# An audio tower on one core: the loops of `pipeline` and `rounds` written out

## The chip, the core and the metric

The kernel runs on one core of a Trainium2 chip. The metric is the time of one execution on the device, in microseconds (us). Each engine of the core runs its own program: TensorE (PE, with its weight loads shown as PEld), VectorE (DVE), ScalarE (ACT), GpSimd (POOL) and SyncE (SP), which here only issues DMA transfers. The engines are ordered against each other by semaphores: an instruction raises one when it is done, another waits until it has reached a value.

## The reference, cut to what matters

The input `x` is 16 batches of 64 channels by 2048 samples. Three stages follow each other.

```python
h = _L0_tok_ref(x, ...)                        # token stage: (16, 128, 1024)
h = h + _L0_attn_ref(_layernorm(h), ...)       # attention stage
h = h + _L0_ffn_ref(_layernorm(h), ...)        # feed-forward stage

# token stage
h = conv1d(x, conv_in_w, pad=3)                # 7 taps, 64 -> 128 channels
h = gelu(groupnorm1(h, gn1_w, gn1_b))
h = conv1d(h, dw_w, stride=2, pad=2, groups=H) + dw_b     # 5 taps, by channel
h = gelu(groupnorm1(conv1d(h, pw_w), gn2_w, gn2_b))       # 128 -> 128

# attention: 32 heads, latent queries (384) and keys (128), rotary part of 64
q_c = rmsnorm(hidden @ w_qa, g_qa); q = q_c @ w_qb
kv = hidden @ w_kva                            # k_c (128, normed) and k_rope (64)
attn = softmax((query @ key.T) * scaling); out = (attn @ v) @ w_o

# feed-forward: a dense layer, and 8 experts of rank 16, the best 2 for each token
out = x @ W_base.T + b_base + sum_of_two_experts(x) * 2
```

## The kernel before, in words

All matrices are split into two halves of 16 bits, a high and a low one (`_h`, `_l`), and most products are made of three matmuls (high by high, low by high, high by low). `resid` holds the running result of all 16 batches in SBUF.

**Token stage** (`token_phase`). One iteration `i` of a pipeline works on several batches at once: the convolution of batch `i`, the first group norm and gelu of `i - 1` (MID), the second of `i - 2` (HID), the layer norm's turned result and the projections of `i - 3` (PROJ), the latents of `i - 4` (TAIL), and the splitting of the input of `i + 2` (AHEAD; `x_high` on ACT, `x_low` on POOL). PE, DVE, ACT and POOL each run `pipeline` (L64) with a body of their own. `pipeline` writes out the iterations at the start and the end, where some of the lags are out of range, and runs the middle, here iterations 4 to 13, as a hardware loop `Fori` whose pass holds two iterations. In the loop the iteration number is a register, and so are the values that waits compare with; in the iterations written out both are constants, and `need` and the bodies' `isinstance(i, int)` leave out waits that can't matter. `wait_apart` (L82) and `Chain` put waits between small operations on one engine. The small steps of the norms on POOL go by `Chain`, as do the sums on DVE (`mean_and_square`). `kr_l` (L405 on DVE) is the last operation of an iteration there. SP loads `x` in a loop of its own (`sp.Fori(1, B)`).

**Attention stage** (`attention_phase`). A round is one group of four heads by one of four quads of batches, 32 rounds in all (`ROUNDS`). A round has four steps `j`. In each step PE makes the scores of one batch for four heads (`scores`, L1068 to L1075, which need `zt`, the rotary queries transposed by DMA), the latent outputs of the step before (`latents`, L1110 to L1112, which need `turned`, the probabilities transposed by DMA), the rotary queries of the next step (`rope`, L1041), a quarter of the queries of the next round (`queries`, L1025), in the first 28 rounds some products of weights for a head four rounds on (`products`), and the output of the step before (`outputs`, L1090 to L1092). DVE and ACT do the softmax and all splitting; SP issues the transposes (L784 `zt`, L791 `turned`), in a loop of its own over all 128 steps (`sp.Fori(1, ROUNDS * QUAD - 1)`). At the start of a round ACT issues the load of another head's weights (`load`, L836), from round 0 to round 26. `rounds` (L758) sets the order for PE, ACT and DVE: round 0 written out, rounds 1 to 26 in a loop of two rounds a pass, round 27 written out, rounds 28 to 30 in a loop of one round a pass, round 31 written out. Where the round is a register, `Round` and `fresh` (L660 to L664) compute the slot, group, side, token offset and half that the round needs by register operations on each engine, anew where an operand needs one.

**Feed-forward stage** (`ffn_phase`). One iteration for each batch: SP transposes the normed input and stores the result, DVE routes, PE multiplies. All five engines run `pipeline`, with iterations 2 to 13 (SP, ACT, DVE) or 2 to 15 (PE, POOL) in the loop.

Of the kernel before, what the change touches and what calls it, by code (L numbers as in the profile page):

```python
# [22 lines left out]
B, CI, T, CH = 16, 64, 2048, 128  # L23
# [11 lines left out]
HEADS = 4  # L35
# [3 lines left out]
ROUNDS = GROUPS * QUADS  # L39
# [22 lines left out]


def pipeline(eng, body, first, lags, steady, unroll=2):  # L64

    assert steady >= max(lags)
    lo, hi = steady, B + min(lags)
    hi -= (hi - lo) % unroll  # L70
    for i in range(first, lo):
        body(i, i % 2, lambda lag, i=i: 0 <= i - lag < B)
    with eng.Fori(lo, hi - unroll + 1, unroll) as r:
        for u in range(unroll):
            body(r + u if u else r, (lo + u) % 2, lambda lag: True)
    for i in range(hi, B + max(lags)):
        body(i, i % 2, lambda lag, i=i: 0 <= i - lag < B)


# [39 lines left out]
def token_phase(nc, keep, raw_loaded, x_d, wc_d, wqk_d, pw_d, rows_d, params_d, consts_d, heads_d):  # L119
# [4 lines left out]
    with ExitStack() as ctx:  # L124
# [101 lines left out]
        def _(act):  # L226
# [95 lines left out]
            weights_high("wc")  # L322
            act.wait_ge(zeroed, ZEROED)
            pipeline(act, body, AHEAD, lags, TAIL)

        @block.gpsimd
        def _(pool):
# [67 lines left out]
            pool.wait_ge(zeroed, ZEROED)  # L395
            pool.wait_ge(w_loaded["params"], 16)
            pipeline(pool, body, AHEAD, lags, TAIL)

        @block.vector
        def _(dve):  # L400
# [152 lines left out]
            dve.wait_ge(zeroed, ZEROED)  # L553
            dve.wait_ge(w_loaded["params"], 16)
            pipeline(dve, body, -1, lags, TAIL)

        @block.tensor
# [155 lines left out]
def attention_phase(nc, keep, raw_loaded, heads_d):  # L713
# [3 lines left out]
    with ExitStack() as ctx:  # L717
# [40 lines left out]
        def rounds(eng, start, body):  # L758

            def run(t, more, parity=None):  # L760
                def at(k):
                    if isinstance(t, int) and not 0 <= t + k < ROUNDS:
                        return None
                    return Round(eng, t + k if k else t, parity if k == 0 or parity is None else 1 - parity)

                body(at(-1), at(0), at(1), more)

            start()
            run(0, True)
            with eng.Fori(1, ROUNDS - HEADS - 2, 2) as t:  # L770
                run(t, True, 1)
                run(t + 1, True, 0)
            run(ROUNDS - HEADS - 1, True)
            with eng.Fori(ROUNDS - HEADS, ROUNDS - 1) as t:
                run(t, False)
            run(ROUNDS - 1, False)

        @block.sync
        def _(sp):
# [22 lines left out]
        def _(act):  # L802
# [52 lines left out]
            def body(before, now, after, more):  # L855
# [25 lines left out]
                if not after:  # L881
                    latent_high(now.slot + (QUAD - 1), False)

            rounds(act, start, body)

        @block.vector
        def _(dve):
# [67 lines left out]
            def body(before, now, after, more):  # L955
# [33 lines left out]
                if not after:  # L989
# [3 lines left out]
                    dve.wait_ge(out_added, ROUNDS * 8)  # L993

            rounds(dve, start, body)

        @block.tensor
        def _(pe):
# [115 lines left out]
            def body(before, now, after, more):  # L1114
# [18 lines left out]
                if not after:  # L1133
                    latents(now, QUAD - 1)
                    outputs(now, QUAD - 1)

            rounds(pe, start, body)


# [350 lines left out]
```

## Time and profile before

| | before |
|---|---|
| median of 3 runs | 2132.52 us (2131.76 to 2133.24) |
| the profiled execution | 2130.34 us |
| its span, first to last instruction | 2128.6 us |
| PE busy | 1938.4 us, 91% of the span, 11794 matmuls |
| DVE busy | 1314.6 us, 62% |
| ACT busy | 757.9 us |
| POOL busy | 279.4 us |
| mean granted TensorE clock | 0.974 of full speed |

The profile is of one execution. A busy time counts an engine's own instructions; register, branch, semaphore and DMA-issuing instructions are not counted as busy. Matmuls overlap, so a busy PE is not PE at its peak. Idle time before an instruction is put down to what ended it; "issue" means that nothing which the profile shows was waited for.

### The profile page before, as it was taken

The numbers are of one execution on the slowest core, as the hardware profiler recorded it, in microseconds if no ns is written. First come the engines' busy times: TensorE is split into PE (matmuls) and PEld (weight loads), VectorE is DVE, ScalarE is ACT, GpSimd is POOL, SyncE is SP. The second block draws the span as 40 slices with busy tenths as digits, with TensorE's granted clock in tenths as the row PEclk, the third lists the DMA queues.
The fourth block names the chain that finished last, engine by engine and source line by source line (L and its number), as shares of the span: only waits on it lengthen the run. The fifth ranks groups of instructions, "written<-read, shape, count | busy, mean of one in ns | idle before, by whom it ended". The sixth has DMA issues, their size and how long they took to land. (4 is left out here: it accounts for less than half of the span.)

```text
span 2128.6 us, 42839 instructions
## 1 busy us (share of the span) xinstructions
PE 1938.4 (91%) x11794; PEld 1066.4 (50%) x11794; DVE 1314.6 (62%) x2805; ACT 757.9 (36%) x2051; POOL 279.4 (13%) x612
## 2 busy tenths in 40 slices
PE   4788888768999999999999999999999999959999
PEld 1344445444555555555555555555555555525554
DVE  3666666635666666666666666666666666656664
ACT  3344444323333333333333333333333333332221
POOL 2354444320000000000000000000000000023332
PEclk8899999979999999999999999999999999979999
DMA  5112211003332222222232222322222121243332
GB/s 137 40 40 47 49 42 38 19 3 95 55 68 55 55 55 69 54 52 54 55 73 55 55 52 54 69 55 55 55 67 55 37 43 38 40 137 75 83 80 69
DMA packets 250560, 123.82 MB, mean 58 GB/s; under 512 B 240272, under 2 KB 240528, under 8 KB 248336
## 3 DMA queue, kind: packets, MB, share of 16 engines
q1 hardware_dynamic: 246192, 94.71, 20.7%
q10 hardware_dynamic: 4320, 28.51, 4.3%
q8 instruction: 25, 0.41, 0.1%
q14 instruction: 23, 0.19, 0.0%
HBM read 56.07 MB, written 8.39 MB: 30 GB/s over the span
## 5 line engine op out<-in xcount | busy, mean ns | idle before, releaser
L1090 PE MATMUL out_ps<-m_h,ot_h 128*128 (+1 forms) x1024 | 389.0, 380 | 4.1 <-DVE ot_l L889 4.1
L1092 PE MATMUL out_ps<-m_h,ot_l 128*128 (+1 forms) x1024 | 388.8, 380 | 0.0
L1091 PE MATMUL out_ps<-m_l,ot_h 128*128 (+1 forms) x1024 | 388.7, 380 | 0.0
L939 DVE SCALAR_TENSOR_TENSOR resid<-out_ps,resid 128x512 f32 (+1 forms) x256 | 177.1, 692 | 309.7 <-PE out_ps L1092 308.6
L804 ACT ACTIVATE ot_h<-av_ps 128x512 f16<-128x512 f32 x128 | 76.4, 597 | 762.5 <-PE av_ps L1112 762.5
L1281 POOL MEMSET fpower<- 128x1 f32 x1 | 0.1, 99 | 1426.3 <-POOLq L717 1426.3
L868 ACT ACTIVATE prob<-s_ps,nmx 128x128 f32<-128x128 f32 x512 | 180.1, 371 | 5.7 <-DVE nmx L965 5.7
L1090 PEld LDWEIGHTS out_ps<-m_h,ot_h 128*128 128x128 f16 x1024 | 100.4, 98 | 129.9 <-issue 13.9
L1091 PEld LDWEIGHTS out_ps<-m_l,ot_h 128*128 128x128 f16 x1024 | 100.4, 98 | 129.5 <-issue 19.1
L1092 PEld LDWEIGHTS out_ps<-m_h,ot_l 128*128 128x128 f16 x1024 | 100.3, 98 | 121.2 <-issue 0.8
L960 DVE TENSOR_REDUCE mx<-s_ps 128x4 f32<-128x512 f32 x128 | 88.5, 692 | 63.9 <-PE s_ps L1075 63.9
L889 DVE SCALAR_TENSOR_TENSOR ot_l<-av_ps,ot_h 128x512 f16<-128x512 f32 x128 | 88.5, 692 | 63.3 <-ACT ot_h L804 63.3
L889 DVE SCALAR_TENSOR_TENSOR halves<-prob,halves 128x512 f16<-128x512 f32 x128 | 88.6, 692 | 59.5 <-ACT halves L804 59.5
L1025 PE MATMUL qp_ps<-qct_h,wp_h 128*128 (+1 forms) x378 | 103.3, 382 | 21.1 <-issue 21.1
L868 ACT ACTIVATION_READ_ACCUMULATOR prob<-s_ps,nmx 128x1 f32 x512 | 109.0, 213 | 0.0
L1025 PE MATMUL qp_ps<-qct_h,wp_l 128*128 (+1 forms) x378 | 102.5, 380 | 0.0
L1025 PE MATMUL qp_ps<-qct_l,wp_h 128*128 (+1 forms) x378 | 102.2, 379 | 0.0
L1394 PE MATMUL fout<-wb_h,fht_h 128*128 128x512 f16 x256 | 97.1, 379 | 0.0
L1394 PE MATMUL fout<-wb_l,fht_h 128*128 128x512 f16 x256 | 97.1, 379 | 0.0
L1394 PE MATMUL fout<-wb_h,fht_l 128*128 128x512 f16 x256 | 97.1, 379 | 0.0
L804 ACT ACTIVATE halves<-prob 128x512 f16<-128x512 f32 x128 | 80.6, 630 | 44.3 <-DVE prob L973 44.3
L1068 PE MATMUL s_ps<-kct_h,qp_h 128*128 (+1 forms) x512 | 92.4, 219 | 0.4 <-DVE qp_l L889 0.4
(239 smaller groups left out, 4014.5 us busy)
## 6 DMA issues: line engine op xcount, KB each, us to landing
wide<-heads_in ACTq DMA_DIRECT2D x30, 928.0 KB, 5.4
wide<-x_in SPq DMA_DIRECT2D x32, 512.0 KB, 6.0
tower_out<-result SPq DMA_DIRECT2D x16, 512.0 KB, 2.6
stage<-wb_in SPq DMA_DIRECT2D x8, 512.0 KB, 8.3
resid<-wqk_in SPq DMA_DIRECT2D x1, 2304.0 KB, 11.8
zt<-z SPq DMA_TRANSPOSE x128, 2.4
turned<-halves SPq DMA_TRANSPOSE x128, 3.0
wide<-heads_in SPq DMA_DIRECT2D x2, 928.0 KB, 4.6
```

The costliest lines, as they stand in the source:

```text
L804: act.activation(out, src, ACT.Copy, scale=scale).then_inc(done, 1)
L868: act.activation(prob[:, h, :], s_ps[:, h * P:(h + 1) * P], ACT.Exp, bias=nmx[:, h:h + 1], scale=EXP_SCALE, accum_out=rsum[:, h:h + 1]).th ...
L889: dve.scalar_tensor_tensor(out=out, in0=src, scalar=scale, in1=high, op0=ALU.mult, op1=ALU.subtract).then_inc(done, 1)
L939: dve.scalar_tensor_tensor(out=resid[:, at], in0=out_ps[hf][:, :], scalar=1.0 / (O_S * M_S), in1=resid[:, at], op0=ALU.mult, op1=ALU.add). ...
L960: dve.tensor_reduce(mx[:, :], s_ps[:, :].rearrange("p (h n) -> p h n", h=HEADS), AX.X, ALU.max).then_inc(max_step, 1)
L1025: last = pe.matmul(bank[:, :], w[:, bass.ds(side, 1), k, j, :].rearrange("p a n -> p (a n)"), q[:, k, bass.ds(tok, CHUNK)], start=n == 0, ...
L1068: pe.matmul(out[h], q_h[h], k_h, start=h == 0, stop=False)
L1090: pe.matmul(out_ps[hf][:, :], ot_h[:, h, :], m_h[:, at], start=h == 0, stop=False)
L1091: pe.matmul(out_ps[hf][:, :], ot_h[:, h, :], m_l[:, at], start=False, stop=False)
L1092: last = pe.matmul(out_ps[hf][:, :], ot_l[:, h, :], m_h[:, at], start=False, stop=h == HEADS - 1)
L1281: pool.memset(power[:, :], -0.5).then_inc(powered, 1)
L1394: pe.matmul(out_ps[p][hf][:, :], h[p][:, k, :], w[:, k, hf * CHUNK:(hf + 1) * CHUNK], start=k == 0 and n == 0, stop=False)
```

## The change

`pipeline` no longer has a middle part: each iteration from `first` on is written out by the program that builds the kernel, with its number as a constant. `rounds` does the same for the 32 rounds. The `Fori` loops of both are gone, on every engine that calls them; SP's own two loops, in the token and the attention stage, stay. The operations and their order on each engine are as before.

```diff
 def pipeline(eng, body, first, lags, steady, unroll=2):
-    assert steady >= max(lags)
-    lo, hi = steady, B + min(lags)
-    hi -= (hi - lo) % unroll
-    for i in range(first, lo):
-        body(i, i % 2, lambda lag, i=i: 0 <= i - lag < B)
-    with eng.Fori(lo, hi - unroll + 1, unroll) as r:
-        for u in range(unroll):
-            body(r + u if u else r, (lo + u) % 2, lambda lag: True)
-    for i in range(hi, B + max(lags)):
+    for i in range(first, B + max(lags)):
         body(i, i % 2, lambda lag, i=i: 0 <= i - lag < B)
...
             start()
-            run(0, True)
-            with eng.Fori(1, ROUNDS - HEADS - 2, 2) as t:
-                run(t, True, 1)
-                run(t + 1, True, 0)
-            run(ROUNDS - HEADS - 1, True)
-            with eng.Fori(ROUNDS - HEADS, ROUNDS - 1) as t:
-                run(t, False)
-            run(ROUNDS - 1, False)
+            for t in range(ROUNDS):
+                run(t, t < ROUNDS - HEADS)
```

## Rows read from the trace of the kernel before

**Rows 1.** Windows, attention rounds: stretch, width, busy us (instructions) by engine, PE clock, DMA
```profile
541.40:631.70 90.30, 85.45 (x541) 47.22 (x540) 55.98 (x120) 31.71 (x104) 0.00 (x0) 1.00 0.31 57
...
631.70:1684.20 1052.50, 1019.32 (x6482) 567.20 (x6481) 670.04 (x1440) 377.48 (x1248) 0.00 (x0) 1.00 0.26 57
1684.20:1726.50 42.30, 41.99 (x272) 23.56 (x271) 27.91 (x60) 15.69 (x52) 0.00 (x0) 1.00 0.20 38
1726.50:1845.00 118.50, 118.50 (x782) 66.34 (x781) 78.33 (x168) 42.27 (x144) 0.00 (x0) 1.00 0.22 40
```

**Rows 2.** Windows (PE, PEld, DVE, ACT, POOL), the loop of the feed-forward stage
```profile
1949.10:2107.20 158.10, 158.10 (x949) 82.11 (x948) 95.42 (x226) 34.14 (x48) 58.41 (x106) 1.00 0.31 80
```

**Rows 3.** Waits of PE, 631.7 to 1684.2: total us, times, longest us
```profile
PE qp_ps L1025 <- issue: 18.9, 24, 0.8
PE s_ps L1074 <- DMA zt<-z: 9.6, 23, 0.6
PE av_ps L1110 <- DMA turned<-halves: 3.9, 19, 0.2
```

**Rows 4.** Timeline of PE in round 27: start, us, instruction [idle before, releaser]
```profile
1695.62 0.38 PE L1110 MATMUL av_ps<-turned,kc_h 128*128 128x512 f16 x1 [0.31 <-DMA turned<-halves]
1695.84 0.38 PE L1111 MATMUL av_ps<-turned,kc_l 128*128 128x512 f16 x1
```

**Rows 5.** Timeline of PE in round 17, first query matmuls
```profile
1250.44 0.81 PE L1025 MATMUL qp_ps<-qct_h,wp_h 128*128 x3 [0.78 <-issue]
```

**Rows 6.** Source line L663 (`fresh`), whole span: ns min/median/max, first and last start
```profile
L663 PEldq FUSED_REGOPS  x584: 47/157/245, 542.4 to 1836.9; - x195
```

**Rows 7.** Timeline of ACT, the load of a head at the turn to round 18
```profile
1284.96 0.35 ACTq L836 DMA_DIRECT2D wide<-heads_in  x1
```

**Rows 8.** Tile `zt`, 1284.5 to 1285.5: its transpose and its landing
```profile
L784 SPq DMA_TRANSPOSE zt<-z x1: 1191/1191/1191, 1284.7 to 1284.7; - x1
...
DMA to landing us min/median/max: 6.0/6.0/6.0
```

**Rows 9.** DMA, 631.7 to 1684.2: all queues with packets; issues, median us to landing
```profile
q1 hardware_dynamic: 154649, 38.03, 19.3%
q10 hardware_dynamic: 3331, 21.92, 6.6%
...
zt<-z SPq DMA_TRANSPOSE x96, 2.4
```

**Rows 10.** DMA, 1684.2 to 1767: instruction queues, packets, MB, share of 16 engines
```profile
q8 instruction: 5, 0.08, 0.4%
q14 instruction: 4, 0.03, 0.1%
```

**Rows 11.** DMA, 541.4 to 631.7 (rounds 1 and 2): instruction queues
```profile
q8 instruction: 6, 0.10, 0.5%
q14 instruction: 3, 0.02, 0.1%
```

**Rows 12.** Tile `zt`, 1690 to 1690.5: the transpose on SP's queue, ns
```profile
L784 SPq DMA_TRANSPOSE zt<-z x1: 2252/2252/2252, 1690.0 to 1690.0; - x1
```

**Rows 13.** Tile `zt`, 580.5 to 581.5: landing of the one transpose there
```profile
DMA to landing us min/median/max: 7.9/7.9/7.9
```

**Rows 14.** Windows, token stage: nine loop steps, then two steps written out
```profile
132.30:361.17 228.87, 195.86 (x1062) 108.28 (x1062) 149.13 (x315) 105.14 (x172) 108.56 (x253) 0.96 0.18 41
361.17:408.54 47.37, 38.45 (x224) 22.07 (x224) 32.61 (x70) 19.76 (x36) 19.91 (x55) 1.00 0.12 41
```

**Rows 15.** Source line L87 (waits of `wait_apart`), POOL: ns min/median/max
```profile
L87 POOLq FUSED_REGOPS  x375: 37/46/57, 107.5 to 2095.8; - x188
```

**Rows 16.** Timeline of DVE: `kr_l` at 132.30, 361.17 and 408.54
```profile
132.30 0.29 DVE L405 SCALAR_TENSOR_TENSOR kr_l<-turn_ps,kr_h 128x128 f32 x1 [3.14 <-ACT kr_h L319]
...
361.17 0.29 DVE L405 SCALAR_TENSOR_TENSOR kr_l<-turn_ps,kr_h 128x128 f32 x1 [3.10 <-ACT kr_h L319]
...
408.54 0.29 DVE L405 SCALAR_TENSOR_TENSOR kr_l<-turn_ps,kr_h 128x128 f16<-128x128 f32 x1 [2.85 <-ACT kr_h L319]
```

## The prediction, made blind

> **What bounds the kernel now.** The page comes first: its first part names TensorE as by far the busiest engine, VectorE next. Those are means over three stages, so I then cut the span into windows, one for each stretch in which a loop runs and one for each stretch of the same work that is already written out. The reader should compare their width with PE's busy time. The loop over attention rounds 3 to 26 takes 1052.50 us for 24 rounds, 43.85 us each, with PE busy for 42.47 of them; round 27, which the kernel before already writes out on PE, ACT and DVE, takes 42.30 us with PE busy for 41.99; rounds 28 to 30, which have no products and still run in a loop, are 118.50 of 118.50 us busy [rows 1]. The loop of the feed-forward stage is full too: 158.10 of 158.10 us [rows 2]. So there is nothing to gain in rounds 28 to 30 and in the feed-forward loop, where PE never waits for a register; what can be gained lies in rounds 1 to 26 and in the token stage.
>
> In the 24 rounds PE has three idle groups: 18.9 us before `qp_ps` L1025 with "issue" as the cause, 9.6 us before `s_ps` L1074 for the transposed `zt`, 3.9 us before `av_ps` L1110 for `turned` [rows 3]. By round these are 0.79, 0.40 and 0.16 us. The idle time of PE understates a stall: matmuls of that shape last 0.38 us and start 0.22 us apart [rows 4], so each stop costs about 0.16 us more than is shown.
>
> The "issue" stall comes once a round, 0.78 us ahead of the first query matmul [rows 5]. It is the helper `fresh` (L663): 584 fused register operations on PE's queue, median 157 ns [rows 6]. Where `queries` turns to the next round's registers, several of these operations follow each other with no matmul between.
>
> The `zt` stall belongs to another cause. At the turn of each round ACT issues the load of another head's weights [rows 7]; the `zt` transpose issued beside it lands after 6.0 us [rows 8], where the median of the 96 is 2.4 us [rows 9]. PE needs that `zt` at the start of the round. The load stays in the changed kernel, so most of this stall is not the loop's.
>
> **The change, part by part.** The sum is made against the profiled execution, 2130.3 us (span 2128.6); the median of the runs is 2132.5, so I add 2.2 us at the end.
>
> *Attention, rounds 1 to 26: registers and back edges removed.* The nearest row is round 27, 42.30 us [rows 1]. It contains one stop of its own, 0.31 us idle before L1110 [rows 4], with the restart 0.47 us, so a round without any stop is 42.30 - 0.47 = about 41.85 us. Round 27 lacks one thing that rounds 1 to 26 have, the load. What the load costs in the loop is 0.40 + 0.16 us idle and two restarts, 0.85 us [rows 3, 4]. In the trace the load is issued 0.3 us after `zt` (1284.96 against 1284.7) [rows 7, 8], with register moves ahead of it on ACT. Without these I expect it some 0.3 us earlier, and since `zt` lands when the load does, the stall should shrink to about 0.4 us. Bounds: 0.1 and 0.85.
>
> *Attention: instruction blocks added.* This is the price of the change. While the loop runs (631.7 to 1684.2) the DMA view names only queues q1 and q10: not one instruction packet in 24 rounds [rows 9]. Wherever code runs for the first time there are such packets: 5 on q8 and 4 on q14 in the 82.8 us from round 27 on [rows 10], 6 and 3 in rounds 1 and 2 [rows 11], about four and a half a round. Written out, all rounds are of that kind. The packets don't stop PE's queue itself (the rows of round 27 to 30 show no issue stall) but they share DMA engines with the transposes: the `zt` transpose issued at 1690.0 took 2252 ns on SP's queue [rows 12] against 1191 ns for the one at 1284.7 [rows 8], and the `turned` behind it is what PE then waited 0.31 us for [rows 4]. With the load in the way as well it is worse: the `zt` at the turn to round 2, issued at 580.7, landed after 7.9 us rather than 6.0 [rows 8, 13]. From below: round 27 lost 0.47 us to four packets or so, and rounds 28 to 30 nothing to the others; call it 0.2 us a round. From above: rounds 1 and 2 together took 90.30 us [rows 1], 2.6 us more than two later ones, for nine packets, so 0.29 us each and 1.3 us a round; 1.5 with some margin. A packet hurts when it falls into the 7 us or so around the load, one sixth of a round, which four or five packets will do in most rounds without the full 1.9 us each. I take 0.8, between the ends and nearer to rounds 1 and 2, as they alone have load and packets together.
>
> Sum for a round: 41.85 + 0.4 + 0.8 = 43.05 us, 26 rounds 1119.3. Before they took 90.30 + 1052.50 = 1142.8 us [rows 1]. Gain 23.5 us; with the bounds of both terms from 42.15 to 44.2 us a round, that is from 47 us gained to 6 lost.
>
> The Trainium skill (Runtime: NRT & Kernel Launch, Instruction fetch mechanics) has a rule on this: prefetch is sequential, and a taken branch whose target lies outside a window of two blocks stalls for a fetch, which speaks for writing loops out more strongly than I do. The trace disagrees here, since the loop's twelve passes fetched nothing [rows 9]; by the rule twelve further stalls would vanish, each about as long as a q8 packet (0.4% of 16 engines' time in 82.8 us for five, 1.1 us each [rows 10]), and the sum would be near 2082.
>
> *Rounds 28 to 30 and the feed-forward loop.* No stall to remove [rows 1, 2]; new packets meet transposes there that are issued well ahead and no load. I take 0.5 us lost, at most 2.
>
> *Token stage, iterations 4 to 13.* Here PE is not the limit: it is busy for 195.86 of 228.87 us in the loop [rows 14]. One chain goes round through all engines: `kr_l` on DVE, the sums of the next batch, `stat_ps` on PE, the group norm's small steps on POOL, the gelu on ACT, five taps on DVE, the layer norm on POOL, `hid` on ACT, `kr_l` again. Between its links sit register operations for the waits: 375 in all on POOL for L87 alone, median 46 ns, and the like on DVE [rows 15]. `kr_l` runs at 132.30 and 361.17 with nine loop steps between, 25.43 us each; the two steps after, to 408.54, which are written out already, take 23.69 each [rows 16], 1.74 us less. They lack only the load-ahead `x_high` and `x_low`, which in the loop fill gaps on ACT and POOL. Part of the 1.74 us is TensorE's clock: in the loop it is granted at 0.96 of 2.4 GHz on the mean, with falls to 1.2 GHz, and at 1.00 in the two steps [rows 14]. PE has its waits for this chain before each fall, so a shorter chain should see fewer; I don't count on all. I take 1.4 us for ten steps, 14 us; bounds 7 and 17. The chain uses no DMA transposes, so packets cost it nothing.
>
> *What stays.* SP's own loops in the token and attention stages (`sp.Fori` over batches and over the 128 transposes) are not touched, and their register work stays in the path of `zt`. No matmul, copy or load is added or dropped.
>
> Sum: 2130.3 - 23.5 - 14 + 0.5 = 2093.3 us; on the median's footing 2095.5, say 2095.
>
> **The rivals.**
> - *Packets are hidden and the load moves out of the way.* Round 27 nearly shows it, but it has no load. Then a round is 42.1 us, 26 rounds gain 48, the token stage 17: 2132.5 - 65 = about 2068. The page cited above says that crossing a block boundary is mostly hidden, which would be this case; rounds 1 and 2 speak against it.
> - *Attention gives its gain back.* Each round loses its 0.95 us of register stall to packets on the load, that is 1.7 us of packets a round. Only the token stage gains: 2132.5 - 14 = about 2118.
> - *Slower.* The place is the first `zt` of each round. If packets fall on the load in every round as at 580.7, each round pays 1.9 us there and some 0.5 in later steps: 41.85 + 0.4 + 2.4 = 44.65, times 26 is 1161, 18 us more than before; with the token stage at its low bound of 7 the time is about 2143. It decides from 2.25 us of packets a round, where the token gain of 14 is used up. Against it: with a packet every 10 us or so, not every one can fall into those 7 us.
> - *It does nothing.* If the written-out waits cost as much as the registers did, the time stays at 2132; round 27 speaks against it plainly.
>
> **How the numbers follow.** Forecast about 2095 (2082 to 2108): 0.57. Packets hidden: 0.13. Attention gives back: 0.17. Slower: 0.08. No change: 0.05. A measurement of this kernel tells 0.2%, 4.3 us, from no change. So faster 0.87, same 0.05, slower 0.08. The range 2070 to 2124 holds the forecast, the third case and part of the second, and leaves out most of the slower ones.
>
> **What would show each step.** Right: the issue group before L1025 is gone; rounds of about 43 us with PE idle only at L1074 and L1110; instruction packets in every round; the load issued no later than `zt`; steps of about 24 us between `kr_l`. Wrong: "issue" idle on PE at regular places (the fetch itself stalls it), rounds over 43.9 us with a longer `zt` wait, or token steps that stay at 25.4 with the clock still falling.

## The result, and the profile after

The changed kernel takes 2095.93 us (median of 4 runs, 2090.39 to 2096.80) against 2132.14 us before: ratio 0.9825, 95% interval 0.9807 to 0.9842. The prediction was 2095 us, 2070 to 2124. The profiled execution took 2096.29 us for a span of 2094.5 us, 34.0 us less than the profiled one before.

The lines of the helpers moved up: L1025, L1074 and L1110 of before are now L1008, L1057 and L1093, the load L836 is L819, and `kr_l` L405 is L394. The windows that answer to [rows 1] and [rows 14] are, in the order rounds 1 to 26, round 27, rounds 28 to 30, nine token steps that were a loop, and the two after them (columns as in those groups: width, busy us of PE, PEld, DVE, ACT and POOL, clock, DMA):

```profile
528.30:1650.50 1122.20, 1101.87 (x7022) 615.76 (x7021) 725.57 (x1560) 408.19 (x1352) 0.00 (x0) 1.00 0.29 59
1650.50:1692.30 41.80, 41.80 (x271) 23.56 (x270) 27.89 (x60) 15.69 (x52) 0.00 (x0) 1.00 0.20 39
1692.30:1810.80 118.50, 118.50 (x782) 66.23 (x781) 77.91 (x168) 42.27 (x144) 0.00 (x0) 1.00 0.21 41
...
131.99:347.53 215.54, 184.32 (x1062) 104.37 (x1062) 150.11 (x316) 105.22 (x171) 117.31 (x253) 1.00 0.19 45
347.53:394.82 47.29, 38.40 (x224) 22.07 (x224) 32.80 (x71) 19.77 (x36) 20.29 (x55) 1.00 0.12 41
```

Rounds 1 to 26 took 1142.8 us before [rows 1] and take 1122.2 now: 20.6 us gained, 43.16 us a round. The nine token steps took 228.87 us [rows 14] and take 215.54: 13.3 us. The two together are 33.9 of the 34.0 us; the rest of the program moved by 0.1 us. The clock in the token steps is 1.00 where it was 0.96.

PE's waits in rounds 1 to 26, which answer to [rows 3] (total us, times, longest), are these two groups alone:

```profile
PE s_ps L1057 <- DMA zt<-z: 10.2, 13, 1.7
PE av_ps L1093 <- DMA turned<-halves: 9.5, 28, 0.4
```

Over the same 26 rounds of the kernel before ([rows 3] has 24 of them) they were

```profile
PE qp_ps L1025 <- issue: 21.1, 28, 0.8
PE s_ps L1074 <- DMA zt<-z: 12.0, 25, 2.2
PE av_ps L1110 <- DMA turned<-halves: 4.1, 20, 0.2
```

The "issue" group is gone. The wait for `zt` is little shorter, but comes half as often: 6.6 of its 10.2 us now fall on four rounds, 1.6 to 1.7 us in each. The wait for `turned` has more than doubled. The DMA view of the same stretch, which answers to [rows 9], now has instruction packets (packets, MB, share of 16 engines), some two of PE's (q8) in each round:

```profile
q8 instruction: 56, 0.92, 0.3%
q14 instruction: 30, 0.25, 0.1%
...
wide<-heads_in ACTq DMA_DIRECT2D x25, 928.0 KB, 5.3
```

They don't cost all rounds the same. A round is counted here from its first score matmul to the next round's. Twenty-two rounds take 42.3 to 43.3 us; rounds 6, 12, 18 and 24 take 44.2, 45.8, 45.8 and 45.8. Rounds 11 and 12 as windows, in the columns of the first fence:

```profile
957.60:999.90 42.30, 41.95 (x271) 23.57 (x270) 27.90 (x60) 15.70 (x52) 0.00 (x0) 1.00 0.27 59
999.90:1045.80 45.90, 43.94 (x272) 24.27 (x271) 27.99 (x60) 15.79 (x52) 0.00 (x0) 0.96 0.31 56
```

Ahead of round 12 the load is issued at 995.02 (from ACT's timeline: start, us), 0.04 us before the `zt` transpose at 995.06, and that `zt` lands after 7.3 us (from the view of the tile); ahead of round 11, with the same 0.04 us, it took 5.5:

```profile
995.02 0.33 ACTq L819 DMA_DIRECT2D wide<-heads_in  x1
```
```profile
L767 SPq DMA_TRANSPOSE zt<-z x1: 1189/1189/1189, 995.1 to 995.1; - x1
...
  PE s_ps L1057: 1.6, 1
...
DMA to landing us min/median/max: 7.3/7.3/7.3
```

The DMA view of the 1.2 us from the start of round 12 on, 999.9 to 1001.1, has one packet of PE's instructions, while `zt` was still on its way. The same stretch of round 11 has none.

```profile
q8 instruction: 1, 0.02, 4.8%
```

So three things were to be tested: whether the two gains are apart from each other, what in a round costs the 1.3 us above a round without stops, and what makes the token steps shorter.

### The profile page after: what moved, and what is told of

Same layout as the page of the kernel before. It is cut to its first block and busy times, and to the rows that moved or that the text cites. A ratio compares the mean times of both kernels' runs of the same rounds, so it can differ in the third digit from the quotient of the medians.

```text
span 2094.5 us, 33517 instructions
## 1 busy us (share of the span) xinstructions
PE 1924.3 (92%) x11794; PEld 1064.8 (51%) x11794; DVE 1310.3 (63%) x2805; ACT 755.6 (36%) x2051; POOL 286.4 (14%) x612
## 3 DMA queue, kind: packets, MB, share of 16 engines
q1 hardware_dynamic: 246192, 94.71, 21.7%
## 5 line engine op out<-in xcount | busy, mean ns | idle before, releaser
L1073 PE MATMUL out_ps<-m_h,ot_h 128*128 128x512 f16 x1024 | 388.2, 379 | 4.1 <-DVE ot_l L872 4.1
L1075 PE MATMUL out_ps<-m_h,ot_l 128*128 128x512 f16 x1024 | 388.1, 379 | 0.0
L1074 PE MATMUL out_ps<-m_l,ot_h 128*128 128x512 f16 x1024 | 388.1, 379 | 0.0
L922 DVE SCALAR_TENSOR_TENSOR resid<-out_ps,resid 128x512 f32<-128x512 f32 x256 | 177.0, 691 | 285.4 <-PE out_ps L1075 281.4
L1074 PEld LDWEIGHTS out_ps<-m_l,ot_h 128*128 128x128 f16 x1024 | 100.2, 98 | 129.2 <-issue 18.6
L1008 PE MATMUL qp_ps<-qct_h,wp_h 128*128 128x512 f16 x378 | 104.8, 387 | 0.0
L1008 PE MATMUL qp_ps<-qct_h,wp_l 128*128 128x512 f16 x378 | 102.7, 381 | 0.0
L1008 PE MATMUL qp_ps<-qct_l,wp_h 128*128 128x512 f16 x378 | 102.1, 379 | 0.0
L1051 PE MATMUL s_ps<-kct_h,qp_h 128*128 128x128 f16 x512 | 92.4, 219 | 0.4 <-DVE qp_l L872 0.4
```

Of the source, the lines that this page charges most:

```text
L922: dve.scalar_tensor_tensor(out=resid[:, at], in0=out_ps[hf][:, :], scalar=1.0 / (O_S * M_S), in1=resid[:, at], op0=ALU.mult, op1=ALU.add). ...
L1008: last = pe.matmul(bank[:, :], w[:, bass.ds(side, 1), k, j, :].rearrange("p a n -> p (a n)"), q[:, k, bass.ds(tok, CHUNK)], start=n == 0, ...
L1051: pe.matmul(out[h], q_h[h], k_h, start=h == 0, stop=False)
L1073: pe.matmul(out_ps[hf][:, :], ot_h[:, h, :], m_h[:, at], start=h == 0, stop=False)
L1074: pe.matmul(out_ps[hf][:, :], ot_h[:, h, :], m_l[:, at], start=False, stop=False)
L1075: last = pe.matmul(out_ps[hf][:, :], ot_l[:, h, :], m_h[:, at], start=False, stop=h == HEADS - 1)
```

## Experiments on the two parts

**The token stage alone, and the rounds alone.** On the kernel before, a copy of `pipeline` without its loop serves the token stage's four engines, or `rounds` is written out, and nothing else:

```diff
+def pipeline_out(eng, body, first, lags, steady, unroll=2):
+    for i in range(first, B + max(lags)):
+        body(i, i % 2, lambda lag, i=i: 0 <= i - lag < B)
...
-            pipeline(act, body, AHEAD, lags, TAIL)
+            pipeline_out(act, body, AHEAD, lags, TAIL)
```

> The kernel before, with only the token stage's batch pipelines written out on all four engines. Theory (the change's gain is the sum of two parts that don't touch): the token stage gains about 13 us, as between the two traces, and the attention rounds keep their 43.85 us each, so about 2132 - 13 = 2119 us; kr_l steps fall from 25.4 to about 23.9 us, and no fall of PE's clock between 113 and 396 us. Rival (the gain of the attention rounds needs the token stage to be written out too, or the token's gain is lost later, since rounds that start elsewhere collide otherwise): outside 2115 to 2123 us.

Measured: 2120.45 us, ratio 0.9938 (0.9917 to 0.9960) to the kernel before at 2133.53 on the same chip, so the time came as expected. The clock did not: the profile has three falls, at 280.67, 304.57 and 328.46 us, and nine token steps in 218.05 us.

> The kernel before, with only the attention rounds written out on PE, ScalarE and VectorE; the token and feed-forward pipelines stay loops. Theory: the rounds gain 20.6 us, as between the two traces, and the token stage nothing, so about 2111 us, rounds of 43.16 us in the mean; the load is issued right before the zt transpose, and instruction packets of PE come back in every round. The slow rounds (44.2 to 45.8 us in the changed kernel: 6, 12, 18 and 24) stay six rounds apart, but may fall on other rounds, since PE has run another number of instructions by then. Rival (the slow rounds belong to the rounds' own work or loads): they stay 6, 12, 18 and 24.

Measured: 2111.86 us, ratio 0.9903 (0.9877 to 0.9928). The two gains, 13.1 and 21.7 us, add to 34.8; the changed kernel gained 36.2. The parts are apart. And the slow rounds moved: with the rounds alone written out they are 3, 9, 15 and 21 (43.7 to 45.9 us). Rounds 9 and 15 of that kernel, behind all of its rounds 1 to 26:

```profile
543.10:1661.50 1118.40, 1098.76 (x7021) 614.29 (x7020) 725.45 (x1560) 408.10 (x1352) 0.00 (x0) 1.00 0.29 59
886.40:930.80 44.40, 42.10 (x271) 23.56 (x270) 27.89 (x60) 15.70 (x52) 0.00 (x0) 1.00 0.30 59
1144.80:1190.80 46.00, 43.93 (x272) 24.29 (x271) 27.99 (x60) 15.70 (x52) 0.00 (x0) 0.96 0.30 56
```

**PE's rounds alone.** As before, but `rounds` is written out for PE only (`rounds(pe, start, body, True)`), so ScalarE keeps its loop and issues the load behind `zt`.

> The kernel before, with the attention rounds written out on PE alone; ScalarE and VectorE keep their loops, so the load of the next head is still issued by ScalarE after its register work, 0.3 to 0.6 us behind the zt transpose. Theory A (PE's own register work is all of the gain, and PE's instruction packets the loss): 0.7 to 0.95 us less in each round for the issue stall, the same packets, so about 2111 us, as with all three engines. Theory B (the load's earlier issue is part of the gain or of the loss): if the zt transpose that starts ahead of the load lands in 6.0 us or less, the rounds become shorter than with all three engines, 2105 us or less; if the load behind it costs more in the turned transposes, longer, 2116 us or more.

Measured: 2117.71 us (2109.87 to 2119.67), ratio 0.9933 (0.9911 to 0.9954); the profiled execution is the fastest of the four. In it the load is issued 0.28 and 0.62 us behind `zt` by turns, rounds 1 to 26 take 1119.3 us against 1118.4 with all three engines written out, and PE's waits are

```profile
PE s_ps L1078 <- DMA zt<-z: 16.6, 24, 2.1
PE av_ps L1114 <- DMA turned<-halves: 4.3, 21, 0.3
```

20.9 us together against 19.4 (9.6 and 9.8) with all three engines. In the same stretch the DMA view has

```profile
q8 instruction: 57, 0.93, 0.4%
q14 instruction: 3, 0.02, 0.0%
```

where the changed kernel has 56 and 30, so the packets on q8 are PE's. The profile speaks for theory A: half a microsecond in the load's place moves waiting between `zt` and `turned` and saves nothing. The median, 6 us above the three engines' with intervals that overlap, leans to the slower half of theory B. That stays open.

## Experiments on the round: load and instruction packets

**The load cut in four.** The changed kernel, with the round's 928 KB in four pieces by columns, one at the start of each step, and PE's wait for the load counting all four:

```diff
-            def load(h, p):
-                act.dma_start(raws[p][:, 0:RAW], heads_d[bass.ds(h, 1), :, :].rearrange("a p n -> (a p) n")
+            def load(h, p, part=None):
+                lo, hi = (0, RAW) if part is None else (part * RAW // 4, (part + 1) * RAW // 4)
+                act.dma_start(raws[p][:, lo:hi], heads_d[bass.ds(h, 1), :, lo:hi].rearrange("a p n -> (a p) n")
...
-                    load(now.t + HEADS + 1, 1 - now.parity)
                 for j in range(QUAD):
                     s = now.slot + j
+                    if more and (not now.known or now.t + HEADS + 1 < NH):
+                        load(now.t + HEADS + 1, 1 - now.parity, j)
```

> The changed kernel with each round's load of 928 KB cut in four loads of 232 KB by columns, one issued at the start of each of the round's four steps instead of all at the first. Theory (what a round has left above 41.85 us is the load lying on the zt and turned transposes, and an instruction packet of PE that comes on top of both in every sixth round): the first zt lands in about 3 us instead of 5.5 to 7.3, the rounds 6, 12, 18 and 24 are like the others, no fall of PE's clock between 510 and 1800 us, rounds of 42.0 to 42.4 us, so about 20 to 30 us less than the changed kernel: 2066 to 2076 us. Rival 1 (the instruction packets alone hold PE up, without the load): rounds stay near 43 and the time at 2090 or more. Rival 2 (four loads hit four zt and four turned transposes instead of one, and each is late by a little): no gain or a loss, 2095 us or more.

Measured: 2063.62 us, ratio 0.9675 (0.9659 to 0.9691), below the 2066 to 2076 us expected. Its rounds 1 to 26, PE's waits in them, and the DMA view of the same stretch:

```profile
536.30:1627.40 1091.10, 1089.82 (x7022) 613.49 (x7021) 725.72 (x1560) 408.09 (x1352) 0.00 (x0) 1.00 0.30 61
```
```profile
PE av_ps L1096 <- DMA turned<-halves: 1.2, 5, 0.3
```
```profile
q8 instruction: 56, 0.92, 0.3%
q14 instruction: 31, 0.25, 0.1%
...
wide<-heads_in ACTq DMA_DIRECT2D x103, 232.0 KB, 2.7
zt<-z SPq DMA_TRANSPOSE x104, 3.2
```

A round takes 41.96 us in the mean, 41.86 in most, with the same 56 packets on q8 as in the changed kernel. So with the load cut the packets cost 0.1 us a round, and the other 1.2 us (43.16 - 41.96) need the whole load. Both rivals fall. A packet still delays a `zt` here: in rounds 6, 12, 18 and 24, where one of PE's starts 1.3 to 2.3 us ahead of the round, that `zt` lands 5.6, 4.9, 5.2 and 4.8 us after its issue, and in the other rounds after 3.2 to 3.8. But PE reaches its first `zt` matmul 5.5 us after the issue, so only round 6, with 42.3 us, pays for it. With the whole load `zt` takes 5.4 us or more in every round, so that time is used up.

**The same cut on the kernel before.**

> The kernel before with the same cut of the load in four, loops kept: the price of the load alone, where PE has no instruction packets in rounds 4 to 25. Theory: PE's wait for zt (9.6 us) and for turned (3.9 us) in rounds 1 to 26 goes, and little else, while ScalarE gets three more sets of address registers and DMA issues in a round: 13 us less at most, 2119 to 2127 us. Together with the changed kernel this gives the parts of a round: without packets and without the load's collision, with either, with both. Rival (the issue stall behind the register work covers the same time as the load's wait): less than 4 us gained.

Measured: 2094.24 us, ratio 0.9824 (0.9808 to 0.9840): as much as the whole change, three times the most I had expected. Rounds 1 to 26 and PE's only wait in them:

```profile
543.30:1646.90 1103.60, 1093.17 (x7021) 612.86 (x7020) 726.00 (x1560) 408.34 (x1352) 0.00 (x0) 1.00 0.29 59
```
```profile
PE qp_ps L1028 <- issue: 10.4, 28, 0.6
```

The waits for `zt` and `turned` are gone, as expected. What I had not expected is that the register stall shrinks too, to 0.40 us a round (0.55 and 0.22 by turns) from 0.79 [rows 3], though the register operations are still there. Their place shows why. First the kernel before in round 17, ahead of the stall of [rows 5]: the operations of L663 on PE's queue (ns min, median, max; first and last start), and PE's first matmul that uses `zt`:

```profile
L663 PEldq FUSED_REGOPS  x6: 93/200/240, 1247.0 to 1249.8; - x6
```
```profile
1246.98 0.23 PE L1074 MATMUL s_ps<-kr_h,zt 128*128 x1 [0.39 <-DMA zt<-z]
```

Then the same round with the load cut, with the first query matmul as well:

```profile
L663 PEldq FUSED_REGOPS  x6: 93/200/240, 1223.0 to 1225.7; - x6
```
```profile
1223.53 0.22 PE L1077 MATMUL s_ps<-kr_h,zt 128*128 x1
...
1226.32 0.81 PE L1028 MATMUL qp_ps<-qct_h,wp_h 128*128 x3 [0.55 <-issue]
```

Six operations of the same lengths over 2.7 to 2.8 us, but with the late `zt` they begin as the `zt` matmul begins, and with the cut load 0.5 us ahead of it. In the program the wait for `zt` stands ahead of these operations on the same queue; while the queue waits, it can't get ahead of the matmuls. Whether it is the size of the four pieces or their place in the round that lets `zt` land in time, these runs don't tell apart.

The four kernels make a table of the mean round in us, and the two causes overlap in it:

| | load whole | load cut in four |
|---|---|---|
| loops | 43.95 | 42.45 |
| written out | 43.16 | 41.96 |

**The packets' place moved.** The changed kernel with 128 more PE instructions before the attention, half of one of PE's packets of 16 KB (in rounds 1 to 26, 14,043 matmuls and weight loads and 390 waits went with 56 packets, about 258 to a packet):

```diff
+                if i >= 16:
+                    for _ in range(32):
+                        pe.sem_inc(pad, 1)
```

> The changed kernel with 128 more PE instructions in the token stage (increments of a semaphore that nobody waits for, 32 in each of the last four iterations, where PE waits for VectorE anyway): half of one of PE's instruction packets of 16 KB, so the packets fall half a period earlier in all that follows. Theory (a round is slow when a packet falls in its first microsecond, on the zt transpose and the load): the slow rounds move from 6, 12, 18 and 24 by three, to 3, 9, 15 and 21, as they lay in the kernel before with the rounds alone written out; the time is 2090 to 2100 us. Rival (the slow rounds belong to the heads or to the load): they stay.

Measured: 2097.89 us, ratio 0.9847 (0.9831 to 0.9864). The slow rounds are 3, 9, 15 and 21 now (44.1, 45.9, 43.9, 43.8). Rounds 6, 9 and 12 of this kernel:

```profile
747.30:789.80 42.50, 42.12 (x271) 23.57 (x270) 27.91 (x60) 15.70 (x52) 0.00 (x0) 1.00 0.29 60
874.70:920.60 45.90, 43.89 (x272) 24.24 (x271) 28.01 (x60) 15.69 (x52) 0.00 (x0) 0.96 0.30 58
1005.80:1048.70 42.90, 42.33 (x272) 23.61 (x271) 27.91 (x60) 15.70 (x52) 0.00 (x0) 1.00 0.27 61
```

The slow rounds follow the count of PE's instructions, not the heads. The start times of the packets in five traces say the same: those of the changed kernel, of this one, of the next, and of the kernels with the rounds written out alone, on three engines or on PE. In 20 of their 130 rounds a packet on q8 starts between 0.2 us before the round's start and 0.9 us after it; these take 43.7 to 45.9 us, with a `zt` that lands after 6.8 to 7.7 us. In the other 110 the rounds take 42.3 to 43.4 us and `zt` 5.4 to 6.7. With 56 packets in 26 rounds, 2.15 a round, a packet comes 0.15 of a period earlier each time, so one falls on the round's start in every sixth or seventh. The 128 instructions turned that by three rounds and left the time as it was.

**SyncE's loops written out as well.**

```diff
-            with sp.Fori(1, B) as b:
+            for b in range(1, B):
...
-            with sp.Fori(1, ROUNDS * QUAD - 1) as s:
+            for s in range(1, ROUNDS * QUAD - 1):
```

> The changed kernel with SyncE's own two loops (the token batches' loads and stores, and the attention's zt and turned transposes) written out too. Theory: SyncE's register work stands between its waits and its issues, so a transpose would be issued some 0.1 to 0.3 us earlier; PE waits for zt and turned in few rounds, so 0 to 5 us less than the changed kernel, 2090 to 2096 us. Rival (SyncE then takes instruction packets of its own, which come on top of its transposes): slower than the changed kernel, 2098 us or more.

Measured: 2097.49 us (2090.76 to 2101.07), ratio 0.9829 (0.9807 to 0.9852): nothing gained that can be measured, between the theory's range and the rival's. Its rounds are 42.94 us, with the slow ones again at 6, 12, 18 and 24, but at 44.1 to 44.3 us, since none of them had a fall of the clock. By that comparison each fall in the changed kernel's slow rounds cost 1.6 us. Its token steps gave back more than the rounds gained (225.83 us for nine, clock 0.92), which leads to the next part.

## Experiments on the token stage

**VectorE's pipeline alone.**

```diff
-            pipeline(dve, body, -1, lags, TAIL)
+            pipeline_out(dve, body, -1, lags, TAIL)
```

> The kernel before, with only VectorE's token pipeline written out; PE, ScalarE and GpSimd keep their loops. Theory (the chain between two kr_l passes crosses all four engines and each of them has register work on it): VectorE's share is what its own pieces lost, dw to lv 0.4 us and the copies 0.1 to 0.3 us, some 0.5 us a step over 10 steps, so about 2127 us (2125 to 2129). Rival 1 (VectorE alone bounds the steps): all 13 us, 2119 us. Rival 2 (the chain's other engines set the step, VectorE's register work runs while it waits): 2132 us.

Measured: 2132.78 us in the median of ten runs, ratio 0.9993 (0.9975 to 1.0010), but three of the ten lie at 2119.5 to 2123.8 us with a mean clock of 0.972 to 0.976, the other seven at 2128 to 2136 with 0.961 to 0.969. The profiled one is the fastest, with nine token steps in 219.10 us. By the median rival 2 would be right, by the profile rival 1. The clock had to be taken out.

**PE's idle time filled.** Each token step has one long idle stretch of PE, mostly 2.3 to 2.7 us before the `stat_ps` matmul, and where the clock fell in a step, it fell within 1.6 us of the end of that stretch (from 2.4 to 1.2 GHz at 183.84 us, with SyncE's loops written out, where PE's idle time ended at 183.81). Ten matmuls whose output nobody reads fill it:

```diff
+                    need(pe, s_copied, i - 1, LAST + HID)
+                    if ok(0) and ok(TAIL):
+                        for _ in range(10):
+                            pe.matmul(stat_ps[:, 4:512], wc_h[:, 0, :], x_h[p][:, 0:508], start=True, stop=True)
                     need(pe, st1_ready, i * 2, 2 * B)
                     need(pe, st2_ready, (i - HID) * 2 + 2, 2 * B)
-                    need(pe, s_copied, i - 1, LAST + HID)
```

> The kernel before, with ten matmuls of 508 columns in each full iteration of the token stage (into columns of stat_ps that nobody reads) at the place where PE stands idle for 2.3 to 2.7 us ahead of the stat_ps matmul; their time is about 10 x 0.216 = 2.2 us, so they fill the idle time and should delay nothing. Theory (a fall of PE's clock follows that idle time, and makes the step that it hits about a microsecond longer; the rest of the token stage's gain is register work): no falls between 130 and 380 us, kr_l steps of 24.9 us (as in the undisturbed ones of the kernel before) instead of 25.4, so 5 us less, 2127 us. Rival 1 (the falls are all of the difference between the two kernels' token stages): 23.9 us a step, 2118 us. Rival 2 (the falls have nothing to do with that idle time, or cost nothing): 2132 us or more.

Measured: 2129.31 us against 2132.75, ratio 0.9983 (0.9973 to 0.9992): less of a gain than the theory's 5 us, but clear of rival 2.

> The kernel before with VectorE's token pipeline alone written out, and the same ten matmuls. That kernel without them came out at 2119.5 to 2123.8 us in three of ten runs and at 2128 to 2136 in the others, with a mean clock of 0.972 to 0.976 against 0.961 to 0.969; its profiled run was the fastest, with kr_l steps of 24.15 us and few falls. Theory (VectorE's register work is worth 1.2 us a step, and falls of the clock after PE's idle time take it back in most runs): with the idle time filled all runs lie at 2117 to 2123 us, steps of 24.2 us or less. Rival (the two levels come from elsewhere): both levels stay, median near 2132 us.

Measured: 2122.40 us (2120.47 to 2127.22), ratio 0.9957 (0.9941 to 0.9974). The median is the theory's, but only two of the four runs lie at 2123 us or less, as all should have.

> The changed kernel with the load cut in four, as before, and the same ten matmuls in the token stage. The cut alone gave 2063.6 us, with 2060.3 to 2074.3 over its runs; the profiled run was the slowest, with a fall of the clock in each token step and steps of 24.5 to 26.5 us. Theory: no fall between 130 and 380 us, steps of 23.7 to 24.3 us in every run, 2058 to 2064 us, and a spread of 4 us or less. Rival (the filling work delays the stat_ps matmul or the conversion behind it): steps of 24.5 us or more, 2066 us or more.

Measured: 2063.59 us (2063.30 to 2065.99), ratio 0.9678 (0.9662 to 0.9694). The median is that of the cut load without the filling; the spread is 2.7 us over four runs instead of 13.9 over five. Nine token steps of these three kernels, in this order, each from its own windows:

```profile
132.41:357.94 225.53, 206.86 (x1155) 113.54 (x1153) 148.92 (x316) 106.34 (x172) 119.19 (x253) 1.00 0.19 42
```
```profile
130.83:348.14 217.31, 206.18 (x1152) 113.26 (x1151) 149.03 (x316) 104.70 (x172) 117.36 (x253) 1.00 0.19 44
```
```profile
130.77:346.96 216.19, 203.77 (x1153) 113.01 (x1152) 150.07 (x316) 105.27 (x171) 117.58 (x253) 1.00 0.20 45
```

In all three the clock is at 1.00 through the steps, where the kernel before has 0.96 [rows 14] and the cut load without filling had

```profile
130.97:355.36 224.39, 199.34 (x1062) 110.54 (x1062) 151.21 (x316) 104.80 (x171) 103.84 (x253) 0.92 0.19 43
```

So the 228.87 us of before come down by 3.3 us without the falls, by 8.2 more with VectorE's register work gone, and by 1.1 with that of PE, ScalarE and GpSimd. These are windows of one profile each; by the medians VectorE's part is 6.9 us (2129.31 to 2122.40). Rival 1 of the run with VectorE's pipeline alone was near: with the falls out, VectorE carries most of the register work's gain. The expectation of 24.9 us a step for the filled kernel before was near (24.9 and 25.2 by turns). With the idle stretch filled, the falls in the steps are gone in all three profiles. The stretch alone doesn't always bring one: the changed kernel's profile has 2.4 to 2.7 us of it in each of the nine steps, and no fall. Whether extra matmuls elsewhere in the step would do the same was not tried.

## Why the prediction was right, step by step

**The round without a stop, 41.85 us.** Right: most rounds of the written-out kernel with the cut load take 41.86.

**The register stall gone from the rounds.** Right in its sign; its size was misread. I took the 0.79 us of "issue" and the 0.40 us for `zt` [rows 3] as two causes that lie side by side. Half of the first came from the second, as the late `zt` took the queue's lead away. Of the 1.50 us that cutting the load saves in the kernel before I had given the load 0.85.

**The load's wait, 0.4 us, and the packets, 0.8 us a round.** The sum was near, 1.2 against 43.16 - 41.86 = 1.30, and that is why the term came out at 20.6 us instead of 23.5. That was luck, since its two parts were mis-sized in opposite ways. With the load cut, packets cost 0.1 us; the whole load with packets around it costs 1.2 more. The step that failed is "packets cost as in rounds 1 and 2, in most rounds": they strike hard where one falls in the first microsecond of a round, which is four rounds of 26. Those four cost 181.7 us, 10.7 more than four of the others' mean, (1122.2 - 181.7) / 22 = 42.75, which is 0.4 us a round over all 26, half of the 0.8; three falls of the clock at 1.6 us are 4.8 of that. What is left, 42.75 - 41.86 = 0.9 us in every round, twice the 0.4, goes with the load, for it went when the load was cut; what the packets elsewhere in a round add to it stays open, as no written-out run has the load without packets. The low end of 0.2 rested on a stop in round 27 that I put down to packets: the changed kernel's round 27 has two on q8 and two on q14 as well, and no stop.

**The load issued 0.3 us earlier.** Right (0.04 us before `zt`, before 0.3 or 0.6 behind it by turns), but it saved nothing in all. In the 22 ordinary rounds `zt` landed a little sooner, after 5.8 us in the median against 6.05 before, and PE waited 0.16 us a round for it instead of the 0.40 of [rows 3]. For `turned` it waited 0.37 us instead of 0.16, so the two together are as long as before. With PE alone written out, where the load stays behind `zt`, they were only 1.5 us longer in 26 rounds than with all three engines.

**Token stage, 14 us.** Right: 13.3 for nine steps in the profile, 13.1 us by the medians of the token stage alone. That the profile agrees so well is luck: it has no fall of the clock in those steps, and the same token code took 217.5, 218.1, 224.4 and 225.8 us in the profiles of four other kernels (128 more PE instructions, token stage alone, load cut, SyncE's loops out). The split between register work and clock was left open in the prediction; it is about 9.3 to 3.3, of the register work 8.2 on VectorE. The low bound of 7 was too high: the changed token stage with falls of the clock in most of its steps took 224.39 us in the profile of the cut load, 4.5 us less than before, and 225.83 with SyncE's loops written out, 3.0 us less.

**Rounds 28 to 30 and the feed-forward stage, 0.5 us lost.** Nothing was lost: from round 27 on the kernels take 444.4 us before and 444.0 after, and round 27 alone went from 42.30 to 41.80.

**The rivals.** The 2068 us of "packets are hidden and the load moves out of the way" describe the cut load well, 2063.6; but the load had to be cut for it, the change alone didn't. "Attention gives its gain back" and "slower" needed a packet on the load in all or most rounds. It is each sixth, because 2.15 packets a round make the collision wander; that a count near a whole number would let it stay is argued, not tried.

The Trainium skill (Runtime: NRT & Kernel Launch, Instruction fetch mechanics) calls the crossing of a block boundary mostly hidden. The runs agree for PE's own queue: with 56 packets PE had no issue stall. The price lay elsewhere, in a `zt` that was late already and landed later still with a packet beside it. The Trainium skill (Trainium Kernel Development and Optimization, Key Constraints) says that DMAs issued from the SP, ACT and POOL queues run on the same 16 DMA engines and interleave. It doesn't name instruction packets there; the DMA view counts them as a share of these 16 engines too (q8 had 4.8% of them in the 1.2 us above).

## What to carry to other kernels

Before a loop is written out, look which transfer the stalls beside it wait for: here cutting one DMA in four gave as much as all loops, and the two together 69 us, more than either. A stall with the cause "issue" can be the echo of an earlier semaphore wait on the same queue; see whether the queue's own work begins when that wait ends. When several runs of one kernel lie far apart and the mean clock goes with them, fill the engine's idle stretch before you judge an edit by the median.

## What was not expected of the hardware

- A late transpose doubled a stall of register operations that stood 3 us behind it: 0.79 against 0.40 us a round with the same six operations of 93 to 240 ns.
- One instruction packet of 16 KB in the first microsecond of a round, as a 928 KB load was landing (0.4 to 0.6 us into the round), came with a `zt` that landed after 7.3 us instead of 5.5. In three of four such rounds of the changed kernel, and five of 20 over five kernels, PE's wait was followed by 3.4 us in which the clock was granted at 1.2 instead of 2.4 GHz, 1.6 us more. With the load cut the packets cost 0.1 us a round, since the `zt` that they delay still lands in time in most.
- Extra matmuls in PE's idle time made the token stage faster, by 3.3 us in the kernel before, by keeping the clock at 1.00 instead of 0.96.
